# First attention of a four-layer hybrid network on one Trainium2 core: keys and values numbered eight to a partition

## The chip, the core and the metric

One core of a Trainium2 chip runs the whole network as one program. The metric is device time in microseconds from the first to the last instruction of one execution; lower is better. The engines are TensorE (PE, and PEld for its weight loads), VectorE (DVE), ScalarE (ACT), GpSimd (POOL) and SyncE (SP), which in this kernel issues nearly all DMAs, in program order from one queue.

## The reference, cut to what matters

The network has eight images of 32 x 32 tokens with 192 channels. Its first layer is an attention with 12 heads of 16 channels and relative positions in rows and columns:

```python
qkv = x.reshape(B, N, E) @ Wqkv + bqkv
qkv = qkv.reshape(B, N, nh, hd, 3).transpose(0, 1, 2, 4, 3)
qkv = qkv.reshape(B * nh, N, hd, 3)
q, k, v = (qkv[..., 0], qkv[..., 1], qkv[..., 2])
attn = jnp.einsum('bnd,bmd->bnm', q * scale, k)
r_q = q.reshape(B * nh, H, W, hd)
rel_h = jnp.einsum('bhwc,hkc->bhwk', r_q, Rh)
rel_w = jnp.einsum('bhwc,wkc->bhwk', r_q, Rw)
attn = (attn.reshape(B * nh, H, W, H, W) + rel_h[..., :, None] + rel_w[..., None, :]).reshape(B * nh, N, N)
attn = jax.nn.softmax(attn, axis=-1)
out = attn @ v
```

The reshape to B * nh takes heads as blocks of 1024 rows of 16 channels in the order (token, head) of the projection. So a "head" is 1024 consecutive rows of 16 floats (64 bytes) of an image's projection. The sum over keys doesn't depend on the order in which the keys are numbered, as long as keys, values and relative terms have the same numbering. The other layers (a dilated attention, a landmark attention, experts, a third attention with its own relative terms, routed experts) aren't touched.

## The kernel before, in words

Each layer is a row of stages; a stage has its own buffers and ends with a barrier of all engines. The name of a stage stands ahead of its tiles in the profile.

**flat** (`project_flat`) normalises the input, projects it and stores queries, keys and values to the scratch tensor `scr_flat`.

**L0A** (`project_heads` with kind "L0") runs over eight images. SP's function `load_rows` (L498 to L503) loads queries, keys and values of one image, one DMA of 768 KB each, so that partition p of head j holds the rows t * 128 + p, t from 0 to 7. Each row is 64 bytes long by itself in the source. `empty` (L569) then has ACT regroup the queries and DVE the keys (L572, from head-major to token-tile-major), PE transposes both (L552, 16 transposes each, four to a PSUM bank, eight banks), and ACT and DVE copy the banks to `qT` and `kT` (L594, L596); before the first two banks of an image they wait until the four stores of the image before have landed (L590). SP stores `qT` and `kT` to `scr_q` and `scr_k` (L514). The order on SP's queue is: wait until the queries and keys of image b are regrouped, load the rows of image b + 1, store the queries of b, store the keys of b. Values go straight to the resident tile `VH`.

**L0R** (`relative_terms`) reads the queries back and computes the terms of rows and columns for 32 relative offsets each, which it stores to `scr_rel0` and `scr_rel1`, one row of 1024 queries per offset and head.

**L0B** (`attend`) runs over 96 heads. A head's queries stand in `QS` together with its relative terms; its keys stand in `KS` together with rows of marks (0 or 1), which pick for each key the terms of its row and column. The matmul of both gives scores with the terms added. Each half of the partitions (64 of them) serves 512 keys: 32 partitions with one kind of marks for all 32 rows or columns, 16 with the marks that occur among the half's keys, and 16 for the channels. The list `TERMS` (L666) names, for each half, which pieces of `scr_rel` go to which partitions, as (first partition, axis, first term, number). SP's `load` (L773 to L786) issues one DMA for each piece, one for the queries' channels, and two for the split into bf16 parts; `LOADS` counts them for the wait of POOL, which prepares a head (L909 to L918). PE computes scores twice: once to find the maximum of each query (L953, taken by DVE at L1080), once to be exponentiated (L963, by ACT at L1067), and then the sums over keys (L990). The row of maxima goes through DRAM: PE transposes it, DVE copies it, SP stores it (L818), waits for its landing (L820) and loads it into `QS` (L822) as a part of the second scores; PE waits for it at the start of a head.

SP's order for head H is written out by hand: store the parts of head H + 3 (L795 to L797), the row of maxima of H + 1 (L815 to L822), place the parts of H + 3 (L808 to L810), store the sums of H - 1 (L830), move a piece of the image before (L844), load head H + 5 (L779 to L786). The first and last 12 heads are code written out; the 72 between them are six turns of a loop over 12 heads.

```python
TERMS = [((0, 1, 0, 32), (32, 0, own, 16)) for own in (16, 0)]
LOADS = 16 * (2 + 2 * len(TERMS[0]) + 2)
for dst, ax, first, n in TERMS[h]:
    sp.dma_start(raw[HALF[h] + dst:HALF[h] + dst + n, :],
                 scr[f"rel{ax}"][i3, 3 * first + h3:3 * (first + n - 1) + h3 + 1:3, :])
```

The third attention, L3A to L3B, uses the same functions with kind "L3" and other lists; it isn't changed.

Of the kernel before, what the change touches and what calls it, by code (L numbers as in the profile page):

```python
# [15 lines left out]
NH, D = 12, 16  # L16
P = 128
T = HW // P
# [38 lines left out]
def bc(ap, axis, n):  # L57

    shape = list(ap.shape)
    shape.insert(axis, n)  # L60
    return ap.unsqueeze(axis).broadcast_to(shape)
# [386 lines left out]
def project_heads(nc, kind, X, VH, scr, cst, w):  # L448
# [6 lines left out]
    with Stage(nc, f"{kind}A") as st:  # L455
# [4 lines left out]
        def bank(n):  # L460
            return ring[:, n % NB, :]
# [5 lines left out]
        else:  # L467
            qk = [st.sb(n, [P, NH, T, D]) for n in ("q_rows", "k_rows")]
            qs = [st.sb(n, [P, T, C]) for n in ("q_tok", "k_tok")]
            s_rows = [st.sem("q_rows_loaded"), st.sem("k_rows_loaded")]  # L470
            s_v = st.sem("v_loaded")
            s_tok = [st.sem("q_rows_regrouped"), st.sem("k_rows_regrouped")]
        qT, kT = st.sb("qT", [CG, G, HW]), st.sb("kT", [CG, G, HW])
        first = st.sb("first", [CG, 2])
# [9 lines left out]
        @block.sync  # L484
        def _(sp):
            def load(dst, src):
                sp.dma_start(dst, src).then_inc(s_w, 16)
                nw[0] += 16

            if kind == "L3":  # L490
                for dst, src in ((wq, w["Wq"]), (wk, w["Wk"]), (wv, w["Wv"])):
                    load(dst[:, :, :], src.rearrange("(k c) n -> c k n", k=G))
                load(first[:, 0:1], w["tvk0"])
                load(first[:, 1:2], w["thk0"])
                load(firstv[:, 0, :], w["tvv0"])
                load(firstv[:, 1, :], w["thv0"])

            def load_rows(b):  # L498
                for c in range(3):
                    src = scr["flat"][c, b, :, :].rearrange("t (c d) -> (t c) d", d=D)  # L500
                    dst = qk[c][:, :, :, :] if c < 2 else VH[:, bass.ds(b * NH, NH), :, :]
                    sp.dma_start(dst.rearrange("p j t d -> p (j t) d"),
                                 src.rearrange("(j p) d -> p j d", p=P)).then_inc(s_rows[c] if c < 2 else s_v, 16)  # L503

            def store(b):
                for n, dst, src in ((NK, scr["q"], qT), (NV, scr["k"], kT)):
                    if kind == "L3" and n == NV:
                        sp.wait_ge(s_first, b + 1)
                    else:
                        sp.wait_ge(emptied[0], J // 2 * b + n // 2)  # L510
                        sp.wait_ge(emptied[1], J // 2 * b + n // 2)
                    sp.sem_inc(s_sp, 1)
                    for g in range(G):
                        sp.dma_start(dst[bass.ds(b * NH + 6 * g, 6), :, :].rearrange("h r n -> (h r) n"),  # L514
                                     src[:, g, :]).then_inc(s_qk_out, 16)

            if kind == "L0":
                load_rows(0)
            with sp.Fori(0, B - 1) as b:
                if kind == "L0":  # L520
                    for c in range(2):
                        sp.wait_ge(s_tok[c], b + 1)
                    sp.sem_inc(s_sp, 1)
                    load_rows(b + 1)
                store(b)
            store(B - 1)
            sp.wait_ge(s_qk_out, 64 * B)
            if kind == "L0":
                sp.wait_ge(s_v, 16 * B)
# [39 lines left out]
        def empty(eng, which, b, last):  # L569

            def copy(dst, src):
                return nc.scalar.copy(dst, src) if which == 0 else nc.vector.tensor_copy(dst, src)  # L572

            if kind == "L0":
                eng.wait_ge(s_rows[which], 16 * (b + 1))
                eng.wait_ge(filled, J * b)
                copy(qs[which][:, :, :].rearrange("p t (j d) -> p j t d", j=NH), qk[which][:, :, :, :]).then_inc(s_tok[which], 1)
            for n in range(NQ + which, J, 2):
                if kind == "L3" and not last:
                    if which == 1 and n == NQ + 1:  # L580
                        norm.dve_stats(nc, eng, b + 1)
                    if which == 0 and n == NQ + 4:
                        norm.act_std(nc, eng, b + 1)
                    if which == 1 and n == NQ + 5:
                        norm.dve_tok(nc, eng, b + 1, J * b + 4)
                eng.wait_ge(filled, J * b + n + 1)
                if n < NV:
                    isk, g, f = n >= NK, n % 4 // 2, n % 2
                    if n < NQ + 2:
                        eng.wait_ge(s_qk_out, 64 * b)  # L590
                    dst, src = (qT, kT)[isk][:, g, f * 512:(f + 1) * 512], bank(n)[0:CG, :]
                    scale = (0.25 if isk else 1.0) if kind == "L0" else (1.0 if isk else 0.25)
                    if which == 0:
                        i = nc.scalar.mul(dst, src, scale)  # L594
                    else:
                        i = nc.vector.tensor_scalar(dst, src, scale, None, ALU.mult)  # L596
                    i.then_inc(emptied[which], 1)
                else:
                    t = n - NV
                    copy(VH[:, bass.ds(b * NH, NH), t, :], bank(n)[:, 0:C].rearrange("p (h d) -> p h d", h=NH)).then_inc(emptied[which], 1)  # L600
                if kind == "L3" and which == 1 and n == NV - 1:
                    eng.wait_ge(emptied[0], J // 2 * b + NV // 2)
                    eng.wait_ge(emptied[1], J // 2 * b + NV // 2)
                    nc.vector.tensor_scalar(kT[:, :, 0:1], kT[:, :, 0:1], first[:, 0:1], first[:, 1:2],
                                            ALU.add, ALU.add).then_inc(s_first, 1)
                if kind == "L3" and which == 1 and n == NV + 1:
                    eng.wait_ge(emptied[0], J // 2 * b + NV // 2 + 1)
                    v0 = VH[0:1, bass.ds(b * NH, NH), 0, :]
                    nc.vector.tensor_tensor(v0, v0, bc(firstv[:, 0, :], 1, NH), ALU.add).then_inc(s_fv, 1)
                    eng.wait_ge(s_fv, 2 * b + 1)  # L610
                    nc.vector.tensor_tensor(v0, v0, bc(firstv[:, 1, :], 1, NH), ALU.add).then_inc(s_fv, 1)

        @block.scalar
        def _(act):
            act.wait_ge(s_w, nw[0])

            def image(b, last):
                if kind == "L3":
                    norm.act(nc, act, b)
                empty(act, 0, b, last)  # L620

            if kind == "L3":
                norm.act_std(nc, act, 0)
            with act.Fori(0, B - 1) as b:
                image(b, False)
            image(B - 1, True)

        @block.vector
        def _(dve):
            dve.wait_ge(s_w, nw[0])  # L630

            def image(b, last):
                if kind == "L3":
                    norm.dve(nc, dve, b)
                empty(dve, 1, b, last)

            if kind == "L3":
                norm.dve_stats(nc, dve, 0)
                norm.dve_tok(nc, dve, 0)
            with dve.Fori(0, B - 1) as b:  # L640
                image(b, False)
            image(B - 1, True)
# [7 lines left out]
def attend(nc, kind, VH, scr, cst):  # L650
# [12 lines left out]

    L0 = kind == "L0"
    if L0:
        TERMS = [((0, 1, 0, 32), (32, 0, own, 16)) for own in (16, 0)]  # L666
    else:
        TERMS = [((0, 1, 0, 16), (16, 1, 16, 15), (31, 0, 16, 1), (32, 0, own, 16)) for own in (0, 17)]
    LOADS = 16 * (2 + 2 * len(TERMS[0]) + 2)
    CT = 32 if L0 else 64  # L670
# [6 lines left out]
    with Stage(nc, f"{kind}B") as st:  # L677
# [87 lines left out]
        def _(sp):  # L765
# [7 lines left out]
            def load(H, u, i):  # L773
# [8 lines left out]
                for h in range(2):  # L782
                    for dst, ax, first, n in TERMS[h]:
                        sp.dma_start(raw[HALF[h] + dst:HALF[h] + dst + n, :],
# [2166 lines left out]
def constants():  # L2951

    c = {"ident": np.eye(P, dtype=np.float32)}
    g = np.arange(CG) // 6
    c["gavg"] = ((g[:, None] == g[None, :]) / 6.0).astype(np.float32)
    m = np.arange(HW)
    k = np.arange(32)[:, None]
    c["marksL0"] = key_marks(m % 32 == 31 - k, m // 32 == 31 - k, (16, 0))
    row, col = np.where(m > 0, (m - 1) // 31, -1), np.where(m > 0, (m - 1) % 31, -1)
    c["marksL3"] = key_marks(np.concatenate([col == np.arange(31)[:, None], row[None, :] == 16]), row == np.arange(33)[:, None], (0, 17))  # L2960
    c["tailL0"] = np.zeros((P, T, 16), np.float32)
# [3 lines left out]
    own = (row - side == np.arange(17)[:, None]) & (row >= 0)  # L2965
# [24 lines left out]
def key_marks(both, own, first):  # L2990

    half = [np.concatenate([both[:, 512 * h:512 * h + 512], own[first[h]:first[h] + 16, 512 * h:512 * h + 512],
                            np.zeros((D, 512), bool)]) for h in range(2)]
    return np.concatenate(half).astype(np.float32)
# [98 lines left out]
```

## Time and profile before

| | us |
|---|---|
| median of 3 runs | 7292.61 (7291.99 to 7298.78) |
| the profiled execution, its own time | 7297.02 |
| its span, first to last instruction | 7295.2 |
| PE busy in the span | 6065.1 (83%) |
| DVE busy | 3563.1 (49%) |
| ACT busy | 2624.7 (36%) |
| POOL busy | 2365.9 (32%) |
| DMA packets | 1,088,658, of these 800,389 under 512 bytes |
| bytes moved | 739.86 MB, 101 GB/s in the mean |
| granted TensorE clock, mean | 0.891 |

The sequence of stages with the times that matter here: L0A issues its first loads at 301 us and its last store at 512 us; L0R runs from 518 to about 650 us; L0B from 650 to about 2150 us. How to read the profile: busy times are those of an engine's instructions, without the issuing of DMAs and the waits. The DMA share is the busy time of the packets over that of 16 engines, and can exceed 1, as several packets can be under way in one engine. In a row of the timeline, "x8" is a run of eight alike instructions, and the bracket behind a row tells how long the engine had been idle and who ended that. SPq rows are DMA issues: their duration is the issuing, not the transfer.

### The profile page before, as it was taken

The numbers are of one execution on the slowest core, as the hardware profiler recorded it, in microseconds if no ns is written. First come the engines' busy times: TensorE is split into PE (matmuls) and PEld (weight loads), VectorE is DVE, ScalarE is ACT, GpSimd is POOL, SyncE is SP. The second block draws the span as 40 slices with busy tenths as digits, with TensorE's granted clock in tenths as the row PEclk, the third lists the DMA queues.
The fourth block names the chain that finished last, engine by engine and source line by source line (L and its number), as shares of the span: only waits on it lengthen the run. The fifth ranks groups of instructions, "written<-read, shape, count | busy, mean of one in ns | idle before, by whom it ended". The sixth has DMA issues, their size and how long they took to land. (4 is left out here: it accounts for less than half of the span.)

```text
span 7295.2 us, 126941 instructions
## 1 busy us (share of the span) xinstructions
PE 6065.1 (83%) x42028; PEld 3280.5 (45%) x42028; DVE 3563.1 (49%) x5163; ACT 2624.7 (36%) x3475; POOL 2365.9 (32%) x2168
## 2 busy tenths in 40 slices
PE   5537999999986677666866797999999998879995
PEld 3425333333334233534756572333333333868885
DVE  2214666666644477444454534555555553451212
ACT  2212555555542211121322223555555554112221
POOL 0003555555530364211000014444444443033122
PEclk8758999999998788877875898999999998979997
DMA  2696333333332211100000154333333334747664
GB/s 89 95 158 190 86 89 89 89 89 89 90 66 74 89 58 43 42 0 1 1 1 0 46 177 113 98 101 99 98 98 101 99 98 141 238 176 240 219 228 158
DMA packets 1088658, 739.86 MB, mean 101 GB/s; under 512 B 800389, under 2 KB 971045, under 8 KB 1077702
## 3 DMA queue, kind: packets, MB, share of 16 engines
q1 hardware_dynamic: 1076038, 710.81, 35.7%
q0 software_dynamic: 12288, 25.18, 1.0%
q8 instruction: 140, 2.29, 0.1%
q14 instruction: 192, 1.57, 0.1%
HBM read 463.95 MB, written 278.00 MB: 102 GB/s over the span
## 5 line engine op out<-in xcount | busy, mean ns | idle before, releaser
L1080 DVE TENSOR_REDUCE L3B_nmax<-L3B_R 128x1 f32<-128x1024 f32 x768 | 939.3, 1224 | 678.2 <-PE L3B_R L953 658.5
L1080 DVE TENSOR_REDUCE L0B_nmax<-L0B_R 128x1 f32<-128x1024 f32 x768 | 939.3, 1224 | 466.0 <-PE L0B_R L953 452.5
L1067 ACT ACTIVATE L0B_PT<-L0B_R 128x1024 f32<-128x1024 f32 x768 | 785.4, 1023 | 603.4 <-PE L0B_R L963 566.2
L1067 ACT ACTIVATE L3B_PT<-L3B_R 128x1024 f32<-128x1024 f32 x768 | 785.2, 1023 | 603.3 <-PE L3B_R L963 560.6
L963 PE MATMUL L3B_R<-L3B_QS,L3B_KS 64*128 64x512 bf16 (+1 forms) x6144 | 795.4, 378 | 2.8 <-DVE L3B_nmax L1080 2.8
L963 PE MATMUL L0B_R<-L0B_QS,L0B_KS 64*128 64x512 bf16 (+1 forms) x6144 | 795.1, 378 | 2.8 <-DVE L0B_nmax L1080 2.8
L990 PE MATMUL L3B_O<-L3B_PT,L3B_VA 128*64 128x512 f32 x3072 | 743.7, 605 | 0.0
L963 PEld LDWEIGHTS L3B_R<-L3B_QS,L3B_KS 64*128 64x128 bf16 (+1 forms) x6144 | 267.6, 94 | 525.6 <-DVE L3B_nmax L1080 232.7
L963 PEld LDWEIGHTS L0B_R<-L0B_QS,L0B_KS 64*128 64x128 bf16 (+1 forms) x6144 | 259.8, 94 | 513.2 <-issue 239.8
L990 PE MATMUL L0B_O<-L0B_PT,L0B_VA 128*32 128x512 f32 x3072 | 409.1, 605 | 0.2 <-ACT L0B_PT L1067 0.2
L1395 POOL TENSOR_TENSOR L1B_qk<-L1B_Q,L1B_K 128x1536 f32<-128x1536 f32 x72 | 260.0, 3630 | 414.3 <-ACT L1B_V L1492 284.9
L953 PE MATMUL L3B_R<-L3B_KS,L3B_QS 64*128 64x512 bf16 x1536 | 299.1, 387 | 70.9 <-DMA L3B_QS<-scr_parts 35.6
L2736 ACT ACTIVATE L3F_hidden<-L3F_H,L3F_weights 128x256 f32<-128x256 f32 x474 | 181.4, 482 | 489.3 <-PE L3F_H L2668 489.3
L953 PE MATMUL L0B_R<-L0B_KS,L0B_QS 64*128 64x512 bf16 x1536 | 297.4, 384 | 63.0 <-DMA L0B_QS<-scr_parts 33.6
L990 PEld LDWEIGHTS L3B_O<-L3B_PT,L3B_VA 128*64 128x64 f32 x3072 | 186.5, 136 | 308.7 <-issue 308.7
L2679 PE MATMUL L3F_OUT<-L3F_weights,L3F_hidden 128*128 128x192 f32 x1896 | 321.1, 326 | 0.0
L2679 PEld LDWEIGHTS L3F_OUT<-L3F_weights,L3F_hidden 128*128 128x128 f32 x1896 | 306.3, 190 | 0.3 <-issue 0.3
L924 POOL COPY L3B_VA<-VH 128x128 f32 (+1 forms) x96 | 27.7, 289 | 763.3 <-PE L3B_O L990 763.3
L2663 PE MATMUL L3F_H<-L3F_turned,L3F_weights 128*128 128x256 f32 x948 | 221.2, 384 | 6.4 <-DVE L3F_turned L2852 3.5
L2605 POOL DMA_INDIRECT L3F_xn<-scr_outs,L3F_position x64 | 61.1, 955 | 484.7 <-DMA scr_outs<-L3F_y 375.5
L953 PEld LDWEIGHTS L3B_R<-L3B_KS,L3B_QS 64*128 64x128 bf16 x1536 | 75.8, 95 | 307.0 <-ACT L3B_PT L1067 156.6
L916 POOL TENSOR_TENSOR L3B_raw<-L3B_raw,L3B_QS 128x1024 f32<-128x1024 f32 x96 | 204.1, 2126 | 18.5 <-POOL L3B_QS L915 18.5
(410 smaller groups left out, 9266.2 us busy)
## 6 DMA issues: line engine op xcount, KB each, us to landing
L3F_weights<-in_L3F_w SPq DMA_DIRECT2D x79, 1251.0 KB, 5.8
scr_sumsL<-L3B_OT SPq DMA_DIRECT2D x96, 512.0 KB
L3C_sums<-scr_sumsL SPq DMA_DIRECT2D x96, 512.0 KB, 9.4
scr_rel<-L0R_terms SPq DMA_DIRECT2D x64, 384.0 KB
L0B_raw<-scr_rel SPq DMA_DIRECT2D x192, 128.0 KB
L3B_raw<-scr_rel SPq DMA_DIRECT2D x384, 64.0 KB
scr_flat<-flat_rows SPq DMA_DIRECT2D x48, 384.0 KB, 3.3
L0B_QS<-scr_parts SPq DMA_DIRECT2D x192, 96.0 KB, 2.1
```

Of the source, the lines that this page charges most:

```text
L916: step(nc.gpsimd.tensor_tensor(raw[:, :], raw[:, :], q[:, 0, :], ALU.subtract), s_tq, 2)
L924: nc.gpsimd.tensor_copy(VA[u % 3][:, :, 0:D], VH[:, H, :, :]).then_inc(s_va, 1)
L953: mm = nc.tensor.matmul(pair[:, h, :], QS[u][rows, 0, t * P:(t + 1) * P], KS[u][rows, 0, :], start=True, stop=True)
L963: mm = nc.tensor.matmul(pair[:, h, :], KS[u][rows, side, kp * P:(kp + 1) * P], QS[u][rows, part, f * HQ:(f + 1) * HQ], start=(part == 0), ...
L990: mm = nc.tensor.matmul(O[c * CT:(c + 1) * CT, bank, :], VA[u % 3][:, kp + 4 * h, :], PT[:, (8 * u + slot) % NPT, h, :], start=(kp == 0), ...
L1067: nc.scalar.activation(PT[:, (8 * u + j) % NPT, :, :], score_pair(u, j), ACT.Exp).then_inc(s_exp, 1)
L1080: nc.vector.tensor_reduce(nmax[:, u % 2, t:t + 1], pair.rearrange("p j n -> p (j n)"), AX, ALU.max, negate=True).then_inc(s_mx, 1)
L1395: nc.gpsimd.tensor_tensor(image(prod[m % 2][:, :, :]), bc(q, 1, R3), neighbours(Kp[n % NSET], n, hf, j), ALU.mult).then_inc(s_prod, 1)
L2605: nc.gpsimd.indirect_dma_start(dst, None, scr[f"outs{g}"], bass.IndirectOffsetOnAxis(POS[k][:, t:t + 1], 0)).then_inc(s_gat[t // 4], 16)
L2663: nc.tensor.matmul(H[:, HB[m], HC[m]:HC[m] + TILE], wb[:, m * P:(m + 1) * P], xt[:, 0, :], start=(HC[m] == 0), stop=False, skip_group_chec ...
L2679: mm = nc.tensor.matmul(OUT[:, i % 2, h * C:(h + 1) * C], hm[i % 2][:, m, h * P:(h + 1) * P], wb[:, W2 + m * C:W2 + (m + 1) * C], start=(m ...
L2736: nc.scalar.activation(hm[i % 2][:, m, :], H[:, HB[m], HC[m]:HC[m] + TILE], ACT.Gelu, bias=WB[i % NB][:, B1 + m:B1 + m + 1]).then_inc(s_ge ...
```

## The change

Keys and values are numbered so that partition p holds the rows 8 p to 8 p + 7 of a head, which are 512 consecutive bytes of the source. All three loads of rows take this form. Keys keep the new order in `kT`, in `scr_k` and in `KS`, and values in `VH`. Queries are put back in their natural order when they are copied out of PSUM: the copy writes 128 elements at a stride of eight for each of a bank's four tiles. With the new numbering a half (t below 4, or from 4 on) holds keys of all 32 image rows and of 16 image columns in four groups of four. So the marks and the pieces of terms change: 32 terms of the row axis in one piece, and the 16 of the column axis in four pieces of four. `LOADS` follows from the list: 14 DMAs a head instead of 8.

```diff
@@ load_rows
                     src = scr["flat"][c, b, :, :].rearrange("t (c d) -> (t c) d", d=D)
                     dst = qk[c][:, :, :, :] if c < 2 else VH[:, bass.ds(b * NH, NH), :, :]
-                    sp.dma_start(dst.rearrange("p j t d -> p (j t) d"),
-                                 src.rearrange("(j p) d -> p j d", p=P)).then_inc(s_rows[c] if c < 2 else s_v, 16)
+                    sp.dma_start(dst.rearrange("p j t d -> p j (t d)"),
+                                 src.rearrange("(j p t) d -> p j (t d)", j=NH, p=P)).then_inc(s_rows[c] if c < 2 else s_v, 16)
@@ empty
                     dst, src = (qT, kT)[isk][:, g, f * 512:(f + 1) * 512], bank(n)[0:CG, :]
+                    if kind == "L0" and not isk:
+                        dst = qT[:, g, :].rearrange("c (p t) -> c t p", t=T)[:, 4 * f:4 * f + 4, :]
+                        src = src.rearrange("c (t p) -> c t p", t=4)
@@ attend
     if L0:
-        TERMS = [((0, 1, 0, 32), (32, 0, own, 16)) for own in (16, 0)]
+        TERMS = [((0, 0, 0, 32),) + tuple((32 + 4 * a, 1, 8 * a + own, 4) for a in range(4)) for own in (4, 0)]
@@ constants
-    c["marksL0"] = key_marks(m % 32 == 31 - k, m // 32 == 31 - k, (16, 0))
+    key = T * (m % P) + m // P
+    mine = np.concatenate([8 * np.arange(4)[:, None] + first + np.arange(4)[None, :] for first in (0, 4)]).reshape(32, 1)
+    c["marksL0"] = key_marks(key // 32 == 31 - k, key % 32 == 31 - mine, (16, 0))
```

## Rows read from the trace of the kernel before

**Rows 1.** Windows by stage: busy time of each engine, granted clock, DMA share, GB/s.

```profile
core 0: us, PE busy (x) PEld busy (x) DVE busy (x) ACT busy (x) POOL busy (x), PEclk, DMA share, GB/s
1.00:20.00 19.00, 0.00 (x0) 0.00 (x0) 0.00 (x0) 0.00 (x0) 0.00 (x0) 1.00 1.03 303
301.00:517.00 216.00, 58.70 (x256) 47.36 (x256) 28.23 (x40) 29.24 (x40) 0.00 (x0) 0.54 1.29 146
...
518.00:650.00 132.00, 115.70 (x1024) 114.95 (x1024) 43.78 (x64) 36.90 (x64) 29.12 (x4) 0.94 0.76 234
700.00:2100.00 1400.00, 1374.73 (x11151) 476.15 (x11149) 967.48 (x1014) 809.65 (x831) 784.25 (x833) 1.00 0.38 89
```

**Rows 2.** Waits of L0A, 301 to 517 us: total, times, longest.

```profile
ACT L0A_qT L594 <- DMA scr_k<-L0A_kT: 124.3, 7, 19.0
DVE L0A_k_tok L572 <- DMA L0A_k_rows<-scr_flat: 106.5, 8, 23.8
```

**Rows 3.** Timeline of L0A, one image: start, duration, engine, line.

```profile
349.16 7.91 SPq L502 DMA_DIRECT2D L0A_k_rows<-scr_flat  x1
351.86 1.08 ACT L594 ACTIVATE L0A_qT<-L0A_ring 96x512 f32<-96x512 f32 x2 [17.37 <-DMA scr_k<-L0A_kT]
...
354.49 0.69 DVE L596 TENSOR_SCALAR L0A_kT<-L0A_ring 96x512 f32<-96x512 f32 x1 [0.74 <-PE L0A_ring L552]
...
366.26 0.96 DVE L572 COPY L0A_k_tok<-L0A_k_rows 128x1536 f32<-128x1536 f32 x1 [11.08 <-DMA L0A_k_rows<-scr_flat]
...
377.89 0.59 ACT L594 ACTIVATE L0A_qT<-L0A_ring 96x512 f32<-96x512 f32 x1 [17.41 <-DMA scr_k<-L0A_kT]
```

**Rows 4.** Timeline of L0A: its first load and the last image's query copies.

```profile
301.10 0.38 SPq L502 DMA_DIRECT2D L0A_q_rows<-scr_flat  x1
...
508.61 1.08 ACT L594 ACTIVATE L0A_qT<-L0A_ring 96x512 f32<-96x512 f32 x2 [17.13 <-DMA scr_k<-L0A_kT]
```

**Rows 5.** Tile views of L0R_terms and L0A_qT: duration in ns, least, median, most.

```profile
L430 DVE COPY L0R_terms<-L0R_ring x64: 676/687/689, 531.7 to 646.3; 96x512 f32<-96x512 f32 x64
...
L596 DVE TENSOR_SCALAR L0A_qT<-L0A_ring x16: 676/678/689, 319.5 to 509.2; 96x512 f32<-96x512 f32 x16
```

**Rows 6.** Timeline of SP's queue over one head of L0B.

```profile
1203.96 0.29 SPq L818 DMA_DIRECT2D scr_max<-L0B_max_rows  x1
1205.22 0.53 SPq L822 DMA_DIRECT2D L0B_QS<-scr_max  x2
...
1211.55 0.85 SPq L784 DMA_DIRECT2D L0B_raw<-scr_rel  x2
1212.50 0.37 SPq L786 DMA_DIRECT2D L0B_raw<-scr_q  x1
...
1219.15 0.29 SPq L818 DMA_DIRECT2D scr_max<-L0B_max_rows  x1
```

**Rows 7.** Waits of SP's queue, 890 to 1980 us (L0B's loop).

```profile
SPq L815 <- DVE L0B_max_rows L1086: 175.3, 67, 3.2
```

**Rows 8.** Timeline of SP's queue in the third attention (L3B).

```profile
5208.16 1.81 SPq L784 DMA_DIRECT2D L3B_raw<-scr_rel  x4
5210.06 0.37 SPq L786 DMA_DIRECT2D L3B_raw<-scr_q  x1
```

**Rows 9.** Tile view of L3B_raw: issue of the loads of terms, ns.

```profile
L784 SPq DMA_DIRECT2D L3B_raw<-scr_rel x768: 229/330/1207, 4408.4 to 6064.6; - x192
```

**Rows 10.** Timeline of L0B around the same head: PE and POOL.

```profile
1212.19 1.03 PE L963 MATMUL L0B_R<-L0B_QS,L0B_KS 64*128 64x512 bf16 x8
...
1218.95 0.40 POOL L909 CAST L0B_kq_parts<-L0B_kq 128x256 bf16<-128x256 f32 x1
```

**Rows 11.** Timeline of SP's queue where L0B's loop turns.

```profile
1067.24 0.46 SPq L797 DMA_DIRECT2D scr_parts<-L0B_kq_parts  x1
1068.07 0.30 SPq L818 DMA_DIRECT2D scr_max<-L0B_max_rows  x1
1069.34 0.53 SPq L822 DMA_DIRECT2D L0B_QS<-scr_max  x2
```

## The prediction, made before the changed kernel ran

> **What bounds the kernel now.** The granted clock and busy shares stage by stage come first, from the windows view [rows 1]. Two stages are touched. In L0A (301 to 517 us), which turns rows of the scratch tensor into per-head queries and keys, PE is busy 59 of 216 us at a granted clock of 0.54, while the DMA share is 1.29 at only 146 GB/s: the DMA engines are full and move little, as with very small packets. In L0B, the attention (here 700 to 2100 us), PE is busy 1374.7 of 1400 us and the DMA share is 0.38: PE is the bound. The waits of L0A [rows 2] say that the copies of queries wait 124.3 us in all for the stores of the image before (they queue behind the loads), and the regrouping of keys 106.5 us for its rows. The timeline [rows 3] shows the rhythm: the query copies that are let go by those stores start at 351.86 and at 377.89, one image apart. From the first (351.86) to the last (508.61) [rows 3, 4] there are six images, (508.61 - 351.86) / 6 = 26.1 us each, and the first loads are issued at 301.10, 50.8 us before 351.86 [rows 3, 4].
>
> **Row loads (eight times three DMAs).** One DMA moves 768 KB. Before, it does so in 12,288 runs of 64 bytes; after, in 1,536 runs of 512. Bytes per image: three loads (2.36 MB) and four stores (1.57 MB). The nearest row for a load with packets of such a size is that of the input, 303 GB/s [rows 1] (its runs have 768 bytes). At that rate the loads take 7.8 us and the stores 5.2, 13.0 us per image. That is the lower bound of a period. The upper one is the 234 GB/s of the stage behind L0A [rows 1], which is bound by PE and so understates the DMA: 16.8 us. I take 13.6, near the first, because the runs are a little shorter than the input's. Six images then save 6 x (26.1 - 13.6) = 75 us. The start: about 2 us to the first byte, 5.2 until queries and keys are in, 1 for the regrouping, 2 for the next loads to flow, 7.8 for these, 5.2 for the stores, 1 for their receipt, 24 to 27 us where there were 50.8. I take 26.8, so 24 saved. What stands behind the last query copy stays. Sum for L0A: **99 us less** (106 at 13.0 us, about 76 at 16.8).
>
> The Trainium skill ("DMA: Bandwidth & Descriptors", Specifications) puts 512 bytes as the least transfer at line rate and HBM's limit per core at about 358 GB/s; an image would take 11.0 us by that (an estimate), and L0A would save some 120. No run here shows such a rate: the input's 303 GB/s is below it.
>
> What comes next in L0A, if the DMAs stop being the bound? From the release of the query copies (351.86) to the end of the last key copy (354.49 + 0.69) is 3.3 us [rows 3], then the key store has to be issued and to land, some 5 us: 8.5 us, under 13.6. PE needs 59 / 8 = 7.3 us an image. Both lie beside the transfers, so the DMAs remain the bound and the two hidden chains cost nothing until the period nears 8.5.
>
> **The query copy with a stride.** 16 copies on ACT and 16 on DVE now write every eighth element. In the stage behind, copies of the same size also write with a stride, at 687 ns on DVE, against 678 for the plain one here [rows 5]. I take 0; bounds are 0 and, if the time doubled, 0.7 us in a chain of 8.5 that is covered by 13.6. At nothing either way.
>
> **Relative terms in L0B.** Per half a head had two loads (32 and 16 rows) and gets five (32, and four of 4). The bytes are equal; six more DMAs a head, 576 in all, go out on SP's queue. SP passes one head per 15.2 us (1203.96 to 1219.15 [rows 6]), in which it issues 22 DMAs, stands from 1203.96 to 1205.22 for the landing of the row of maxima, and idles at the end until the next row is ready. That idle time is the cover: in the part that runs in a hardware loop (six turns of 12 heads) it is 175.3 us over 72 heads, 2.43 us each [rows 7]. In the sample head two loads of terms and the step to the next take 0.95 us, 0.475 each [rows 6]; in the third attention, with loads of 16, 15, 1 and 16 rows, four take 1.90, again 0.475 [rows 8]. The cheapest issue there is 229 ns (I take it for a single row's) against a median of 330 [rows 9]; with the 0.145 between two issues (0.475 less 0.330) a DMA can cost as little as 0.37. Between 0.37 and 0.475 I take 0.44, as four rows lie nearer to one than to thirty-two. Six cost 2.64 us (2.2 to 2.85) against 2.43 of idle time. So SP's queue goes from having some room to being **just full**: 0.2 us short per head (0 to 0.42), 15 us in 72 heads (0 to 30). Before PE feels it, the row of maxima may come later: it is fetched from 1205.22 on in two DMAs of 0.53 us together, is in by about 1207 if these need as long as the store before them (1.26), and PE begins the head that needs it at 1212.19 [rows 6, 10], 5 us of room. I count **10 us more** for L0B (0 to 25). The 24 heads at the ends run with code written out, and there SP has more idle time.
>
> Behind the waiting SP stand, in order, the placing of parts, the storing of sums and the loads for the head five ahead; their users come a head or more later, so a delay of some us reaches none of them. POOL starts on the next head at 1218.95 [rows 10], when loads whose issue ended near 1214 are in; with six more DMAs they end near 1217 and are in near 1219. It may start up to 1 us late, and is busy for 784 of 1400 us only [rows 1], so it catches up: 0. Whether the row's round trip grows when it is issued hard behind the stores of parts can be read: at the turn of the loop it is issued 0.37 us after them and still comes back after 1.27 us [rows 11], like in the sample head (1.26 [rows 6]). Nothing for that.
>
> The masks and everything on PE, ACT, DVE and POOL in L0B keep their number and shape: 0.
>
> **Sum.** The profiled execution has 7297.0 us (4.4 above the median of the runs, 7292.6). -99 + 10 = -89 gives 7208 for it, and 7204 against the median.
>
> **Rivals.**
> 1. *SP's queue becomes the bound in earnest.* For it: the idle time and the cost of six DMAs are within 0.2 us of each other, and nothing here shows a load of four rows. Against: at the loop's turn SP has no idle time left already [rows 11], and PE is busy for 98% of the stage all the same. With 0.5 to 0.6 us a DMA it is 0.57 to 1.17 us short per head, 36 to 79 us lost in 72 heads after the 5 of room: 7230 to 7273. Most of this lies at its near end; chance 0.20.
> 2. *The loads stay below the input's rate*, with a period of about 17 to 19 us: reads and stores share the ring. Against: the input's load had no such loss [rows 1], and a share of 1.29 falls with the packet count. The six images save 43 to 55 us and the start 18: 7230 to 7242 with L0B's 10. Chance 0.12.
> 3. *It ends slower: the maxima's row queues.* In each head SP stands still from the store of the maxima until it has landed. If rows of terms in the queue make this round trip 1.26 + 1.8 us, SP is 2.0 us short per head, 72 x 2.0 - 5 = 139 us lost, 40 us slower than before: 7333. It decides from 1.2 us more per trip on (72 x 1.44 = 104). The price is small and the loop's turn speaks against it. Chance 0.04.
> By the Trainium skill ("DMA: Bandwidth & Descriptors", Why a DMA increments its semaphore by 16 and not by 1) a DMA from SP is spread over the largest number of engines up to 16 that divides its outer sizes, the lowest-numbered first, so that the loads of four rows would use four engines each, always the same, which is what could queue the maxima. No row here shows engines one by one.
> 4. *It doesn't do what it says*: the transfers are still cut at 64 bytes. Then L0A stays and L0B costs 10: 7303. Chance 0.04.
>
> **How the numbers follow.** The forecast has 0.60. The range goes from 7184 (106 saved in L0A, nothing lost, a little more at the start) to 7252 (76 saved and 35 lost): it takes in the near half of rival 1 and all of rival 2, and leaves out its far end, rivals 3 and 4. A measurement of this kernel can tell about 0.2%, 15 us, from no change. Faster: 0.60 + 0.20 + 0.12 = 0.92. Same: rival 4, 0.04. Slower: rival 3, 0.04.
>
> **What would show it.** Right: some 258,000 packets under 512 bytes less; L0A's GB/s about 270 and its length near 118 us; query copies 13 to 14 us apart; the strided copies at 0.59 and 0.68 us; SP's idle time before the row of maxima near zero, and L0B within 10 us of its length. Wrong: an unchanged packet count (rival 4); a period over 16 us with a full DMA share (rival 2); PE waiting for the row at the start of each head, with a period of heads above 15.5 us (rivals 1 and 3, told apart by the row's round trip).

## The result, and the profile after

| | before | changed |
|---|---|---|
| median beside each other | 7295.7 us (4 runs) | 7204.0 us (4 runs, 7192.9 to 7210.0) |
| ratio, 95% interval | | 0.9869 (0.9857 to 0.9881) |
| the profiled execution | 7297.0 us | 7192.9 us |

The change makes the kernel 92 us faster by the medians, and 104 us by the two profiled executions; single runs of either kernel differ by some 10 us and more. The stages it touches can be read to a tenth of a microsecond, so the parts are compared there. By the end of L0B's second scores the profiled execution is 98.2 us ahead (2149.0 against 2050.8); the other 6.0 us arise in stages that the change doesn't touch, and no run here explains them. The page of the changed kernel:

```profile
span 7191.0 us, 128381 instructions
...
DMA packets 830609, 739.85 MB, mean 103 GB/s; under 512 B 505477, under 2 KB 712997, under 8 KB 819654
```

The packets fell by 258,049, as the step from 12,288 to 1,536 in 24 DMAs asks (24 x 10,752 = 258,048). The windows by stage, which answer to [rows 1]; columns as there:

```profile
300.00:408.50 108.50, 53.16 (x256) 45.87 (x256) 33.63 (x40) 35.58 (x40) 0.00 (x0) 0.63 0.93 290
409.00:541.00 132.00, 114.49 (x1024) 113.74 (x1024) 43.77 (x64) 36.96 (x64) 29.30 (x4) 0.94 0.77 236
592.00:1992.00 1400.00, 1367.39 (x11080) 473.30 (x11078) 959.88 (x1008) 804.36 (x825) 781.07 (x830) 1.00 0.38 89
324.97:398.56 73.59, 40.18 (x192) 34.27 (x192) 24.97 (x30) 26.32 (x31) 0.00 (x0) 0.64 0.99 313
```

L0A has shrunk from 216 to 108 us and moves 290 GB/s where it moved 146. The last row is its steady part, from the second image's query copies to the last's: a share of 0.99, 313 GB/s. L0B moves and computes as before, but in 1400 us PE is busy 7.3 us less: it waits somewhere. The rhythm of L0A, which answers to [rows 3, 4], first and last:

```profile
300.02 0.38 SPq L502 DMA_DIRECT2D L0A_q_rows<-scr_flat  x1
...
324.97 2.01 ACT L597 ACTIVATE L0A_qT<-L0A_ring 96x512 f32<-96x512 f32 x2 [8.53 <-DMA scr_k<-L0A_kT]
...
398.56 2.01 ACT L597 ACTIVATE L0A_qT<-L0A_ring 96x512 f32<-96x512 f32 x2 [7.37 <-DMA scr_k<-L0A_kT]
```

Six images in 73.6 us are 12.27 us each (26.1 before), and the start takes 24.95 us (50.8). The copies of queries (two in 2.01 us) are longer than before (1.08 us). The tile view of L0A_qT, which answers to [rows 5]:

```profile
L597 ACT ACTIVATE L0A_qT<-L0A_ring x16: 1081/1104/1137, 309.0 to 399.4; 96x512 f32<-96x512 f32 x16
L599 DVE TENSOR_SCALAR L0A_qT<-L0A_ring x16: 1068/1078/1086, 309.8 to 399.5; 96x512 f32<-96x512 f32 x16
```

SP's queue over one head of L0B, which answers to [rows 6]:

```profile
1101.45 0.29 SPq L821 DMA_DIRECT2D scr_max<-L0B_max_rows  x1
1102.71 0.53 SPq L825 DMA_DIRECT2D L0B_QS<-scr_max  x2
...
1109.05 2.11 SPq L787 DMA_DIRECT2D L0B_raw<-scr_rel  x5
1111.26 0.32 SPq L789 DMA_DIRECT2D L0B_raw<-scr_q  x1
1111.71 2.47 SPq L787 DMA_DIRECT2D L0B_raw<-scr_rel  x5
...
1115.89 0.47 SPq L800 DMA_DIRECT2D scr_parts<-L0B_kq_parts  x1
1116.64 0.29 SPq L821 DMA_DIRECT2D scr_max<-L0B_max_rows  x1
```

Between the last store of parts (it ends at 1116.36) and the store of the next row of maxima there are 0.28 us, the bare order of instructions: SP no longer idles there. The waits of SP's queue over the loop's 72 heads (783 to 1880 us), where [rows 7] had 175.3, and then, from the tile views, the terms' loads and the second scores:

```profile
SPq L818 <- DVE L0B_max_rows L1089: 1.4, 3, 0.7
```

```profile
L787 SPq DMA_DIRECT2D L0B_raw<-scr_rel x960: 250/259/1187, 554.6 to 1983.4; - x192
...
L966 PE MATMUL L0B_R<-L0B_QS,L0B_KS x6144: 373/376/631, 590.8 to 2050.8; 64*128 64x512 bf16 x149, 49*128 49x512 bf16 x50
```

The second scores run from 590.8 to 2050.8 us, 1460.0 us; before they ran from 697.7 to 2149.0, 1451.3 us. So L0B gives 8.7 us back. One turn of the loop, from the first row of maxima of a turn to the next turn's:

```profile
1150.27 0.30 SPq L821 DMA_DIRECT2D scr_max<-L0B_max_rows  x1
...
1334.78 0.30 SPq L821 DMA_DIRECT2D scr_max<-L0B_max_rows  x1
```

These are 184.5 us for 12 heads; before it was 182.4 (1068.07 to 1250.50). Who waits because of it shows in the waits of the fourth of the six turns (1335 to 1520 us):

```profile
POOL L0B_kq_parts L912 <- DMA scr_parts<-L0B_kq_parts: 29.5, 9, 3.6
...
PEld L0B_R L956 <- POOL L0B_QS L921: 4.9, 7, 0.7
PEld L0B_R L966 <- DVE L0B_nmax L1083: 4.0, 2, 2.7
PEld L0B_R L956 <- issue: 3.8, 6, 0.7
PE L0B_R L966 <- DMA L0B_QS<-scr_max: 2.2, 1, 2.2
```

In this turn PE waits for the row of maxima once, 2.2 us. The PEld rows are gaps of the weight loads, which overlap PE. Ahead of the first scores (L956) they come to 8.7 us, of which 4.9 end with POOL, which itself waits for SP's stores of parts. In the kernel before, the same gaps are there with nobody to wait for, as its turn from 1250.50 to 1432.66 us shows:

```profile
PEld L0B_R L953 <- issue: 8.5, 12, 0.7
```

So POOL comes late, but no time of PE is seen to be lost by it. The waits of PE itself over the whole of L0B (590 to 2051 us) have one row that the kernel before doesn't have:

```profile
PE L0B_R L966 <- DMA L0B_QS<-scr_max: 6.9, 5, 2.2
```

That is most of the 8.7 us. Four of these five waits (from 1152.53, 1335.55, 1521.63 and 1704.92 us on) begin within 2.3 us of a turn's first row of maxima. SP's queue shows why they lie there:

```profile
1145.18 0.32 SPq L789 DMA_DIRECT2D L0B_raw<-scr_q  x1
1148.44 0.41 SPq L798 DMA_DIRECT2D scr_parts<-L0B_kq_parts  x1
```

Where the loop turns, SP issues nothing for 2.9 to 3.2 us (five times), without a wait in the views; between the same two DMAs of other heads it is 0.33 us as a rule. Without the 2.7 us of difference SP would need (184.5 - 2.7) / 12 = 15.15 us a head (an estimate), no more than PE's 15.2. So what SP lacks, 2.1 us a turn, is less than what the loop's turn costs it. The kernel before has it too (from 1063.11 to 1066.20 us), and there SP's idle time covered it. A loop with more heads in a turn was not tried.

### The profile page after: what moved, and what is told of

It reads as the page before. It is cut to its first block and busy times, and to the rows that moved or that the text cites. A ratio compares the mean times of both kernels' runs of the same rounds, so it can differ in the third digit from the quotient of the medians.

```text
span 7191.0 us, 128381 instructions
## 1 busy us (share of the span) xinstructions
PE 6051.3 (84%) x42028; PEld 3275.3 (46%) x42028; DVE 3567.7 (50%) x5163; ACT 2634.3 (37%) x3475; POOL 2368.7 (33%) x2168
## 3 DMA queue, kind: packets, MB, share of 16 engines
q0 software_dynamic: 12288, 25.18, 1.0%
## 5 line engine op out<-in xcount | busy, mean ns | idle before, releaser
L956 PE MATMUL L3B_R<-L3B_KS,L3B_QS 64*128 64x512 bf16 x1536 | 299.1, 387 | 71.1 <-DMA L3B_QS<-scr_parts 36.5
L956 PE MATMUL L0B_R<-L0B_KS,L0B_QS 64*128 64x512 bf16 x1536 | 297.6, 385 | 66.8 <-DMA L0B_QS<-scr_parts 36.7
L956 PEld LDWEIGHTS L3B_R<-L3B_KS,L3B_QS 64*128 64x128 bf16 x1536 | 75.8, 95 | 307.2 <-ACT L3B_PT L1070 156.5
L381 POOL COPY L3R_q_by_column<-L3R_qT 96x4092 f32<-96x4092 f32 x4 | 30.4, 7631 | 548.6 <-DMA L3R_qT<-scr_q 548.6
```

The source lines that it names most:

```text
L956: mm = nc.tensor.matmul(pair[:, h, :], QS[u][rows, 0, t * P:(t + 1) * P], KS[u][rows, 0, :], start=True, stop=True)
```

## The experiments

**Theory S**: in L0B the cost is SP's time for issuing six more DMAs a head. **Theory D**: L0A is bound by the DMA engines, before by the number of packets and now by the bytes. Rivals to S: the four-row loads themselves (if each used few DMA engines), or the new numbering. Rivals to D: the chain of copies and stores; a step at 512 bytes; one wait that alone made the gain.

**The six DMAs alone, in the kernel before.**

```diff
-        TERMS = [((0, 1, 0, 32), (32, 0, own, 16)) for own in (16, 0)]
+        TERMS = [((0, 1, 0, 32),) + tuple((32 + 4 * a, 0, own + 4 * a, 4) for a in range(4)) for own in (16, 0)]
```

> The kernel before, with old numbering and 64-byte rows, but the 16 own terms of each half loaded in four pieces of four rows: six DMAs more per head on SP's queue, nothing else. Theory S (the cost in L0B is the issuing on SP's queue): a turn of 12 heads takes 184.5 us as in the changed kernel (182.4 before), SP's wait for the row of maxima falls from 175 us to nearly 0 over the 72 heads of the loop, L0B from its first to its last score matmul takes 1460 us (1451 before), the total is 7297 + 9 = 7306 us. Rival N (the new numbering of keys or the queries' stride costs in L0B): 182.4 us a turn and 1451 us, total 7297.

Measured: 7310.5 us beside 7300.9 for the kernel before. SP's waits over the loop, and a turn:

```profile
SPq L815 <- DVE L0B_max_rows L1086: 1.4, 3, 0.7
```

```profile
1075.49 0.29 SPq L818 DMA_DIRECT2D scr_max<-L0B_max_rows  x1
...
1260.00 0.30 SPq L818 DMA_DIRECT2D scr_max<-L0B_max_rows  x1
```

A turn takes 184.5 us, SP's idle time is gone to the same 1.4 us, and the second scores take 1461.3 us (700.9 to 2162.2). The numbering and the stride have no part in L0B's cost. Over the loop this gives the price of a DMA: SP's time a head without its idle time was (182.4 / 12) - (175.3 / 72) = 12.77 us and is 184.5 / 12 - 0.02 = 15.36, so six DMAs cost 2.59 us, 0.43 each.

**The same number of DMAs, each over 16 rows.**

```diff
                     for dst, ax, first, n in TERMS[h]:
-                        sp.dma_start(raw[HALF[h] + dst:HALF[h] + dst + n, :],
-                                     scr[f"rel{ax}"][i3, 3 * first + h3:3 * (first + n - 1) + h3 + 1:3, :]).then_inc(s_ld[u % 2], 16)
+                        for c0 in range(0, HW, 256 if L0 and n == 16 else HW):
+                            c1 = c0 + (256 if L0 and n == 16 else HW)
+                            sp.dma_start(raw[HALF[h] + dst:HALF[h] + dst + n, c0:c1],
+                                         scr[f"rel{ax}"][i3, 3 * first + h3:3 * (first + n - 1) + h3 + 1:3, c0:c1]).then_inc(s_ld[u % 2], 16)
```

> The kernel before, with the own terms of each half loaded in four pieces of 16 rows and a quarter of the queries each: as many DMAs and bytes as the changed kernel has, but each DMA spread over 16 rows. Theory S (issuing on SP): a load of 16 rows takes 0.33 us to issue where one of four rows takes 0.26, so eight of them are 0.5 us a head dearer than in the changed kernel: 190.5 us a turn, L0B about 1495 us, total about 7340. Rival E (loads of four rows sit on few DMA engines and hold up the row of maxima): L0B as before, 1451 us and 182.4 us a turn, total 7297.

Measured: 7355.1 us beside 7300.9. The tile view of the terms' loads, and a turn:

```profile
L786 SPq DMA_DIRECT2D L0B_raw<-scr_rel x960: 311/316/471, 664.8 to 2140.2; - x192
```

```profile
1087.71 0.29 SPq L820 DMA_DIRECT2D scr_max<-L0B_max_rows  x1
...
1279.19 0.30 SPq L820 DMA_DIRECT2D scr_max<-L0B_max_rows  x1
```

A turn takes 191.5 us and the second scores 1501.5 (705.0 to 2206.5). Spreading each load over 16 rows did not help but cost 7 us a turn more. Each such DMA takes 57 ns longer to issue (316 against 259), and eight a head make 5.5 us a turn of that; the rest is not explained, and this run also has 18,431 packets more than the kernel before. The total came out above the 7340 expected. The rival said that L0B would go back to its old length; it became longer. What remains of it, that the four-row loads cost something beside SP's time, is settled by the two runs below that keep them.

**The query copy without its stride.**

```diff
-                    if kind == "L0" and not isk:
-                        dst = qT[:, g, :].rearrange("c (p t) -> c t p", t=T)[:, 4 * f:4 * f + 4, :]
-                        src = src.rearrange("c (t p) -> c t p", t=4)
```

> The changed kernel with the query copy out of PSUM written without the stride, so the queries stay in the order of the keys: leaves out putting the queries in order. Copies go back from 1104 and 1078 ns to 592 and 678. Theory D (L0A is bound by the DMA engines, share 0.99): the period of an image stays at 12.3 us and only the last image's tail is 1 us shorter; total 7192 to 7203. Rival C (the chain stores landed, copies, transposes, stores is the bound): the period falls by 0.7 to 0.9 us to 11.4, L0A by 6 us.

Measured: 7190.5 us. The query copies of the timeline:

```profile
324.92 1.08 ACT L594 ACTIVATE L0A_qT<-L0A_ring 96x512 f32<-96x512 f32 x2 [7.54 <-DMA scr_k<-L0A_kT]
...
398.35 1.08 ACT L594 ACTIVATE L0A_qT<-L0A_ring 96x512 f32<-96x512 f32 x2 [7.05 <-DMA scr_k<-L0A_kT]
```

The copies are short again (1.08 us for two) and the period is (398.35 - 324.92) / 6 = 12.24 us against 12.27: the stride is hidden, and the chain is not the bound.

**Queries in runs of 64 bytes, keys and values in runs of 512.**

```diff
                 for c in range(3):
...
+                    if c == 0:
+                        sp.dma_start(dst.rearrange("p j t d -> p (j t) d"),
+                                     src.rearrange("(j p) d -> p j d", p=P)).then_inc(s_rows[c], 16)
+                        continue
```

and the query copy without its stride, as before.

> The changed kernel without the stride and with the queries' rows loaded in runs of 64 bytes as before, keys and values in runs of 512; queries and keys are then numbered differently, each right in itself. Theory D (each load costs the DMA engines its own time): a third of 26.1 - 12.3 comes back, 4.6 us: 16.9 us an image, and L0A is 6 x 4.6 + 9 = 37 us longer than in the changed kernel. Rival (the gain is a matter of one wait, for instance the keys' rows, DVE's wait before): the period stays near 12.3 or jumps past 20.

Measured: 7242.5 us. The query copies and the window between them:

```profile
334.10 1.08 ACT L598 ACTIVATE L0A_qT<-L0A_ring 96x512 f32<-96x512 f32 x2 [8.35 <-DMA scr_k<-L0A_kT]
...
432.70 1.08 ACT L598 ACTIVATE L0A_qT<-L0A_ring 96x512 f32<-96x512 f32 x2 [7.82 <-DMA scr_k<-L0A_kT]
```

```profile
334.10:432.70 98.60, 41.76 (x192) 35.79 (x192) 21.17 (x30) 21.78 (x31) 0.00 (x0) 0.60 1.15 237
```

16.43 us an image, 4.2 above the changed kernel's: close to a third of 13.9 (4.6), for one of three loads. So the gain is not a matter of one wait; the other two loads were not tried alone.

**Runs of 256 and of 128 bytes.** Each head's part is cut in two or in four pieces, that is j = 24 or 48; the edit for two:

```diff
-                    sp.dma_start(dst.rearrange("p j t d -> p j (t d)"),
-                                 src.rearrange("(j p t) d -> p j (t d)", j=NH, p=P))
+                    sp.dma_start(dst.rearrange("p j (s t) d -> p (j s) (t d)", t=4),
+                                 src.rearrange("(j p t) d -> p j (t d)", j=24, p=P))
```

> The changed kernel with all three loads of rows cut into runs of 256 bytes (four rows) instead of 512; the rows then stand in another order than the marks assume, so the output's numbering is left inconsistent; the work is the same. Theory D (the DMA engines are the bound, each packet costs about 7.5 ns plus its bytes): 576 packets of 18 ns per engine and image in place of 288 of 28: 10.4 + 4.9 for the stores = 15.3 us an image (12.3 with 512, 26.1 with 64). Rival (a step at 512 bytes, below which a packet costs extra): 18 us or more. L0B unchanged at 1460.

> As the run before, with runs of 128 bytes (two rows). Theory D: 1152 packets of 12.7 ns per engine and image: 14.6 + 4.9 = 19.5 us an image. Rival (a step at 512 bytes): 23 us or more. L0B unchanged at 1460.

Measured: 7209.8 and 7238.6 us. The windows of six images, first for 256 bytes, then for 128:

```profile
326.00:410.00 84.00, 40.82 (x192) 34.67 (x192) 24.98 (x30) 26.35 (x30) 0.00 (x0) 0.62 1.07 276
```

```profile
333.80:437.90 104.10, 41.91 (x192) 34.61 (x192) 24.97 (x31) 26.36 (x31) 0.00 (x0) 0.60 1.15 225
```

| run | packets of the loads per DMA engine and image | us an image |
|---|---|---|
| 64 bytes | 2304 | 26.12 |
| 128 | 1152 | 17.35 |
| 256 | 576 | 14.00 |
| 512 | 288 | 12.27 |

The two new sizes came in under what theory D had said (15.3 for 256 bytes, 19.5 for 128), and far under the rival's (18 and 23). Each packet less saves 7.6 ns (64 to 128), 5.8 (128 to 256) and 6.0 (256 to 512): the time falls with the count of packets, and there is no step at 512 bytes. My duration per packet was that of one packet in the trace, and at small sizes several are under way at once (the share is 1.07 and 1.15), so the sum of their durations is more than the time: 1.07 x 14.00 is 15.0 us, and 1.15 x 17.35 is 20.0. The series also shows no flat end: down to 288 packets each one less still saved 6 ns. Longer runs than 512 bytes were not tried, so that the bytes alone are the bound now, as theory D had it, is not shown.

**One DMA a head off SP's queue.** In two ways; first the sums of a head are stored by ACT:

```diff
@@ sync, store_sums
-                    sp.wait_ge(s_on, H + 1)
-                    sp.sem_inc(s_spw, 1)
-                    sp.dma_start(scr["sumsL0"][H, :, :].rearrange("(q p) d -> p q d", p=P), ON[o][:, :, :]).then_inc(s_po[o], 16)
@@ scalar, steps
+                    if j == 5 and L0 and (not isinstance(H, int) or H >= 1):
+                        store_sums(H - 1, u - 1)
+
+            def store_sums(H, u):
+                o = u % 2
+                act.wait_ge(s_on, H + 1)
+                act.sem_inc(s_actw, 1)
+                act.dma_start(scr["sumsL0"][H, :, :].rearrange("(q p) d -> p q d", p=P), ON[o][:, :, :]).then_inc(s_po[o], 16)
```

> The changed kernel with one DMA per head taken off SP's queue: the normalised sums of a head are stored from ACT's queue (after the sixth exponential of the next head). The four-row loads stay. Theory S (SP's queue is full): SP's work falls by about 0.6 us a head, from 15.4 to 14.8, below the 15.2 that PE needs: a turn of 12 heads takes 182.4 us again (184.7 in the changed kernel), SP waits again for the row of maxima, 25 to 35 us over the 72 heads of the loop, L0B takes 1452 us (1460), total 8 to 9 us under the changed kernel. Rival E (the four-row loads themselves hold something up, wherever they are issued): 184.7 and 1460 stay.

Measured: 7180.1 us beside 7289.0. Then the two loads for the parts in one, with both scratch tensors in one:

```diff
-                sp.dma_start(kq[:, 0, :], scr["k"][H, :, :].rearrange("d (c n) -> (d c) n", n=P)).then_inc(s_ld[u % 2], 16)
-                sp.dma_start(kq[:, 1, :], scr["q"][H, :, :].rearrange("d (c n) -> (d c) n", n=P)).then_inc(s_ld[u % 2], 16)
+                sp.dma_start(kq[:, :, :], scr["kq"][:, H, :, :].rearrange("b d (c n) -> (d c) b n", n=P)).then_inc(s_ld[u % 2], 16)
```

> The changed kernel with the two loads of a head's keys and queries for the bf16 parts made one DMA (same bytes, same packets; both scratch tensors lie in one), in L0B and L3B. Theory S: 0.47 us a head less on SP, 14.9 against 15.2 that PE needs: 182.4 us a turn, SP waits 15 to 25 us for the row of maxima in the loop, L0B 1452 us. L3B, where SP has idle time anyway, keeps its length within 1 us. Rival E: 184.7 and 1460 stay.

Measured: 7197.5 us beside 7289.0. SP's waits over the loop, with the sums moved, and with one load:

```profile
SPq L819 <- DVE L0B_max_rows L1097: 41.7, 57, 1.8
```

```profile
SPq L817 <- DVE L0B_max_rows L1088: 15.3, 30, 1.5
```

A turn from the one kernel and from the other:

```profile
1147.03 0.29 SPq L822 DMA_DIRECT2D scr_max<-L0B_max_rows  x1
...
1329.49 0.29 SPq L822 DMA_DIRECT2D scr_max<-L0B_max_rows  x1
```

```profile
1146.20 0.30 SPq L820 DMA_DIRECT2D scr_max<-L0B_max_rows  x1
...
1328.52 0.30 SPq L820 DMA_DIRECT2D scr_max<-L0B_max_rows  x1
```

182.5 and 182.3 us: the turn of the kernel before. The second scores take 1453.4 and 1452.1 us, with the four-row loads in place in both. Two reliefs of a different kind give the same, and SP has idle time left over in both (41.7 us where 25 to 35 were expected, and 15.3 where 15 to 25 were). Theory S stands. With one load L3B changes by 1.2 us (1701.6 to 1700.4), as SP has idle time there (it waits 293.0 us for the row of maxima). The total of this run, 7197.5, lies above that of the other by 17 us although L0B is as short. Of this, 12 us are in L3C (from its first matmul to its last 245.7 us against 233.4) and 5 in L2C (222.5 against 217.5); no edit touches these stages, and single runs differ by as much.

**Five rounds.**

> The changed kernel once more, in five rounds on one chip beside the kernel before: 88 to 104 us less than before, ratio 0.986 to 0.988; a turn of 12 heads 184.7 us.

> The changed kernel with the sums of a head stored from ACT's queue, in five rounds: by theory S 7 to 9 us under the changed kernel (L0B 1453 us instead of 1460, nothing else), so about 97 to 112 us under the kernel before. By the rival that the gain in L0B is taken back in a later stage: the same as the changed kernel within 3 us.

> The changed kernel with both: sums stored from ACT's queue, and one load for the parts' keys and queries. SP then has about 1.1 us a head less to issue. By theory S the second relief brings nothing beyond the first, as PE is the bound again with either: 182.4 us a turn, L0B 1451 to 1453 us, SP's wait for the row of maxima in the loop about 70 us; total within 3 us of the run with the sums alone.

| kernel | median us | ratio to before (7301.6) | 95% interval | second scores, us |
|---|---|---|---|---|
| changed | 7201.9 | 0.9873 | 0.9855 to 0.9891 | 1460.5 |
| with the sums from ACT | 7193.6 | 0.9851 | 0.9830 to 0.9872 | 1452.9 |
| with both | 7179.5 | 0.9848 | 0.9824 to 0.9872 | 1451.7 |

Both versions are faster than the kernel before beyond doubt. Against the changed kernel the intervals overlap, so the totals don't settle it; the stage does, by 7.6 and 8.8 us. The 14 us between the last two medians are not explained by L0B (1.2 us), and the expectation of 3 us was finer than these rounds can tell. SP's wait over the loop was 68.7 us with both, about 70 as expected.

## Why the prediction was right, point by point

The predicted median was 7204, the measured one 7204.0; the agreement to the last microsecond is luck: the profiled execution was forecast at 7208 and took 7192.9, mostly because L0A gave some 9 us more than forecast, and the runs differ by 17 us among themselves. The forecast gain was 89 us; the stages give 98 to 100, and so do the medians of the five rounds (99.7), while those of the first four runs give 92. By its steps:

- **What bounds L0A**: right. The packets were the load; the run with one load in runs of 64 bytes and those with 128 and 256 show that the time goes with their number.
- **The period of an image**: forecast 13.6 between 13.0 and 16.8, measured 12.27, below the lower bound. The term was mis-sized because the input's 303 GB/s was taken for a ceiling; the steady part of L0A moves 313, above it. The start was forecast at 26.8 us and took 24.95. Together: the first matmul of L0R came at 527.9 and comes at 419.1, 108.8 us earlier (1.1 of it from the flat stage), where 99 were forecast and 106 were the bound. The parts of the start (2 us to the first byte, 1 for the receipt and so on) had no rows behind them; only their sum can be compared.
- **The limit by bytes**: the Trainium skill ("DMA: Bandwidth & Descriptors", Specifications) gave 11.0 us an image by its 358 GB/s (an estimate); measured are 12.27 at 313 GB/s, so the measurement stands below that limit. The 512 bytes that the Trainium skill gives there as the least size for line rate show as no step here: runs of 256 bytes already bring 276 GB/s.
- **What is next in L0A**: right. The chain of copies and stores, by the prediction's 8.5 us and the longer copies about 9 us (an estimate), stays hidden: with the short copies the period is the same within 0.03 us.
- **The strided copy**: the size was wrong, the effect right. The rows taken for comparison said 0: in L0R's copies of [rows 5] the turn is in the reading of PSUM, and where they are turned they write four neighbouring elements at a time, while the changed query copy writes single elements 32 bytes apart. That this is what tells them apart is read from the code and was not tried by a run. The copies became 0.51 us (ACT) and 0.40 us (DVE) longer, within the bound of a doubling. The cover named for it holds: without the stride the period is 12.24.
- **SP's queue in L0B**: right in mechanism and size. 0.44 us a DMA was forecast; five loads and the step to the next take 2.21 us (1109.05 to 1111.26), 0.44 each, and over the loop six cost 2.59 us. SP is (184.5 - 182.4) / 12 = 0.18 us short a head where 0.2 was forecast. The idle time went from 175.3 us to 1.4, and 8.7 us are lost where 10 were forecast. What the prediction didn't see, though [rows 11] shows the place, is that SP loses some 3 us at each turn of the loop, and that without them its time would just be enough.
- **Who waits**: right. The prediction put all of the delay on the row of maxima, and PE waits for it 6.9 us of the 8.7. In the loop that is in each of the last four of the six turns (0.7, 2.2, 1.0 and 2.1 us), near the turn's start. The prediction let POOL catch up, and it doesn't quite: over the loop it waited 401.1 us for PE's sums before and 162.0 after, and now waits 192.6 us for SP's stores of parts and 59.5 for its loads. But its lateness falls into gaps of the weight loads that were there before, so 0 was the right price for it.
- **The rivals**: an unchanged cut of the transfers is refuted by the packet count; slow loads by the period; the queueing row of maxima by its round trip, which is still 1.26 us (1101.45 to 1102.71). Packet counts bear on the four DMA engines named there. One load for the parts makes 192 DMAs fewer in all and 3,072 packets fewer, 16 a DMA. The six further DMAs a head, put into the kernel before, left the count as it was (1,088,657 against 1,088,658): eight loads of four rows leave as many of these packets as two of 16 rows, so four each. That fits four engines a load; no row shows the engines one by one. SP's queue as the bound in earnest is what loads of 16 rows would have made: 1501.5 us for the second scores, 50 more than before.
- One number of the signs was named wrongly: the packets in all fell by 258,000, those under 512 bytes by 295,000, as those of 512 no longer count among them.

## What to carry to other kernels

When a stage shows a DMA share at or above 1 and few GB/s, count packets: making the contiguous run longer saved 6 to 8 ns a packet on each DMA engine at every step from 64 to 512 bytes, and it can be done by renumbering an index over which one only sums. The price lies in what is bound to the old order, and should be looked for on the queue that issues DMAs: take its idle time per unit of work and compare it with the added issues at about 0.44 us each. Count in what the issuing engine loses where a loop turns. An issuing queue that has just become full can be relieved by one DMA, as in the two places tried here; a second relief brought about 1 us more in the stage.

## What the runs showed that was not expected

- A copy from PSUM of 96 x 512 floats that writes every eighth element takes 1104 ns on ACT and 1078 on DVE, against 592 and 678 when it writes in order.
- Loads in runs of 256 bytes cost only 1.7 us an image (14 per cent) more than those of 512: 6 to 8 ns for each packet more on each DMA engine, at every size from 64 to 512 bytes.
- A DMA of four rows takes 259 ns to issue on SP, one of 16 rows with a quarter of the columns 316.
- At each turn of the loop of 12 heads SP issues nothing for 2.9 to 3.2 us, against 0.33 us at the same place in other heads. With the queue as full as it is here, SP lacks less than that (2.1 us a turn).
